# Expert rows scattered into a slot-sorted table, read back in column quarters and transposed on VectorE

## The reference

```python
def _moe_forward(hidden_states, Wg, W1, W2, W3, W1s, W2s, W3s):
    x = hidden_states.reshape(-1, D)
    shared = jax.nn.silu(x @ W1s.T) * (x @ W3s.T) @ W2s.T
    probs = jax.nn.softmax((x @ Wg.T).astype(jnp.float32), axis=-1)
    topk_w, sel = jax.lax.top_k(probs, TOP_K)                      # 4 of 16
    combine = jnp.zeros((T, E), x.dtype).at[jnp.arange(T)[:, None], sel].add(topk_w)
    h = jax.nn.silu(jnp.einsum('td,efd->etf', x, W1)) * jnp.einsum('td,efd->etf', x, W3)
    routed = jnp.einsum('etf,edf->td', h * combine.T[:, :, None], W2)
    return (shared + routed).reshape(B, S, D)

x = x + tanh(g_xattn) * attention(layernorm(x), ctx, wq, wk, wv, wo)
x = x + tanh(g_ffn) * moe(layernorm(x), ...)
```

## Time and profile before

| | us |
|---|---|
| median of 3 runs | 1171.72 (1171.42 to 1180.43) |
| the profiled execution's own time | 1170.14 |
| its span, first to last instruction | 1168.5 |
| attention, up to about | 436 |
| routing, about | 436 to 552 |
| experts, about | 552 to 1051 |
| combining, from about | 1051 |

### The profile page before, as it was taken

How to read it: one execution, slowest core, us unless ns; L and a number is a source line. 1 busy time by engine, 2 the same in 40 slices (tenths; PEclk the granted TensorE clock), 3 DMA queues, 4 the chain that set the end, 5 groups by cost and what they waited for, 6 DMA issues and landing times. The chain is left out here.

```text
span 1168.5 us, 18611 instructions
## 1 busy us (share of the span) xinstructions
PE 1106.2 (95%) x5666; PEld 940.0 (80%) x5667; DVE 490.0 (42%) x994; ACT 279.6 (24%) x575; POOL 477.5 (41%) x521
## 2 busy tenths in 40 slices
PE   3999999999999959998989999999999999988997
PEld 3888878878878827686879999999999999977775
DVE  2243463445336255996222222222222222225847
ACT  1231131122113002111223333333333333321210
POOL 4720201201100235101665565556656665617763
PEclk9999999999999968899999999999999999998999
DMA  9411320312220528133864666666666666627785
GB/s 348 193 73 73 122 94 1 141 74 72 108 72 0 225 85 297 36 111 96 325 226 162 216 229 229 238 220 222 236 220 229 229 220 229 215 69 237 226 278 162
DMA packets 54209, 199.70 MB, mean 171 GB/s; under 512 B 7009, under 2 KB 7009, under 8 KB 45985
## 3 DMA queue, kind: packets, MB, share of 16 engines
q0 software_dynamic: 21184, 122.44, 30.1%
q1 hardware_dynamic: 22624, 57.98, 13.9%
q10 hardware_dynamic: 10368, 18.88, 4.3%
HBM read 161.51 MB, written 37.75 MB: 171 GB/s over the span
## 5 line engine op out<-in xcount | busy, mean ns | idle before, releaser
L86 PE MATMUL c_ps_u<-expert_hi,xT_hi 128*128 x576 | 192.7, 335 | 2.0 <-DVE xT_lo L1445 1.9
L86 PE MATMUL c_ps_u<-expert_hi,xT_lo 128*128 x576 | 186.0, 323 | 0.0
L86 PE MATMUL c_ps_u<-expert_lo,xT_hi 128*128 x576 | 185.6, 322 | 0.0
L986 POOL TENSOR_TENSOR expert_lo<-expert_raw,expert_hi (+3 forms) x39 | 158.2, 4079 | 19.9 <-issue 14.0
L73 POOL TENSOR_TENSOR idle<-idle 128x1 f32<-128x1 f32 x91 | 17.5, 192 | 232.0 <-PE c_ps_x L1471 141.3
L86 PEld LDWEIGHTS c_ps_u<-expert_hi,xT_hi 128*128 128x128 f32 x576 | 108.8, 189 | 2.9 <-issue 2.9
L86 PEld LDWEIGHTS c_ps_u<-expert_lo,xT_hi 128*128 128x128 f32 x576 | 109.3, 190 | 0.0
L1459 DVE TENSOR_TENSOR hf<-c_ps_u,gate 128x352 f32<-128x352 f32 x72 | 37.8, 525 | 170.3 <-ACT gate L1434 170.3
L86 PEld LDWEIGHTS c_ps_u<-expert_hi,xT_lo 128*128 128x128 f32 x576 | 108.7, 189 | 0.0
L1449 DVE TENSOR_TENSOR hT_lo<-c_ps_h,hT_hi 128x256 fp32r<-128x256 f32 x72 | 30.6, 425 | 181.4 <-ACT hT_hi L1424 181.4
L86 PE MATMUL c_ps_y<-expert_hi,hT_hi 128*128 (+1 forms) x216 | 91.7, 425 | 2.6 <-DVE hT_lo L1450 2.3
(11 more groups left out here) (268 smaller groups left out, 2454.5 us busy)
## 6 DMA issues: line engine op xcount, KB each, us to landing
expert_hi<-we POOLq DMA_DIRECT2D x16, 1920.0 KB, 7.9
expert_raw<-we POOLq DMA_DIRECT2D x14, 1920.0 KB, 13.0
y_dram<-y ACTq DMA_DIRECT2D x72, 256.0 KB, 2.1
ctxT_hi<-ctxT POOLq DMA_DIRECT2D x4, 1024.0 KB, 7.4
ctxT_raw<-ctxT SPq DMA_DIRECT2D x4, 1024.0 KB, 5.6
ctx_raw<-ctx SPq DMA_DIRECT2D x4, 1024.0 KB, 4.8
r_t<-x SPq DMA_DIRECT2D x4, 1024.0 KB, 5.3
ctx_hi<-ctx POOLq DMA_DIRECT2D x4, 1024.0 KB, 6.9
```

What stands on the lines that cost most here:

```text
L86: last = pe.matmul(out, a[i], b[j], start=(n == 0), stop=(n == 3 * len(pairs) - 1))
L986: last = eng.tensor_tensor(lo, raw, hi, ALU.subtract)
```

## The change

- **A sorted table.** The DRAM tensor `sorted` has a row for every slot. In the attention phase SP fills it with copies of `x` from DRAM to DRAM (24 DMAs of 448 rows, 6 per batch), so that unused slots hold numbers. In the routing phase SP loads the 12 row tiles that are not on the chip yet, and POOL scatters all 2048 rows to their 4 slots each: 64 indirect DMAs. The one-hot matrices, the 64 matmuls and `index` are gone; `counts` and the choice of slots move up in `work`.
- **Loads.** SP, not POOL, brings the tile: 4 DMAs of 32 partitions x 4 x 128 columns, one for each quarter of the columns, after a wait for the whole scatter. The first four tiles are loaded at the end of the routing block, later ones in the expert block behind the zeros. W1 and W3 are laid out to match (`sides`).
- **Transposes.** VectorE transposes 32x32 blocks of `xg` into the new SBUF tile `xt`. ScalarE and VectorE split from `xt` instead of PSUM, one tile ahead (`high(t + 1)`, `low(t + 1)`). PE's `turn` is gone.
- **POOL in the loop** has only the weights' work. Its subtraction is as before one of 3840 columns and one of 512; a wait for `held` comes before it.

```diff
@@ attention_phase, SP
+            def fill(k):
+                for n in range(FILLS):
+                    sp.dma_start(sorted_d[k, n], io["x"][0:SORTED // (B * FILLS)]).then_inc(keep["filled"], 16)
...
                 stores(b - 1)
+                fill(b - 1)
...
+            fill(B - 1)
             sp.wait_ge(m_ready, 22 * B - 10)
@@ routing_phase, SP
             for i in range(IT):
                 sh.load(sp, 1, i)
+            for tile, at in rows.items():
+                if tile // IT != 1:
+                    sp.dma_start(at[:], xn2_d[tile]).then_inc(rows_in, 16)
...
-            sp.wait_ge(keep["gathered"][0], 16)
+            sp.wait_ge(moved, NT * TOPK * 16)
+            sp.wait_ge(sh.u_ready, 2 * SC)
+            for t in range(QUAD):
+                load_tile(sp, mem, later, t, t, keep["loaded"][t])
             load_expert(sp, later.w_raw, WE, io, 1, keep["second_raw_in"])
@@ routing_phase, POOL
+            def move(tile):
+
+                for q in range(TOPK):
+                    pool.indirect_dma_start(mem["sorted"], bass.IndirectOffsetOnAxis(
+                        ap=keep["slots"][:, tile, q:q + 1], axis=0), rows[tile][:], None).then_inc(moved, 16)
+
+            pool.wait_ge(slots_ready, 1)
+            pool.wait_ge(keep["filled"], B * FILLS * 16)
+            for i in range(IT):
+                pool.wait_ge(sh.xs_in[1][i], 16)
+                move(IT + i)
+            pool.wait_ge(rows_in, (NT - IT) * 16)
+            for tile in range(NT):
+                if tile // IT != 1:
+                    move(tile)
+            pool.wait_ge(scheduled, 1)
             pool.wait_ge(sh.t_free, 2 * IT)
-            pool.wait_ge(hot_ready, 1)
+            pool.wait_ge(moved, NT * TOPK * 16)
             load_expert(pool, later.w_hi, WE, io, 1, keep["w_in"])
...
@@ routing_phase, VectorE
-            work = {0: lambda: (rank(), choices()), 1: rest_of_down, 3: counts,
...
+            work = {0: lambda: (rank(), choices()), 1: rest_of_down, 2: counts, 3: slots, 5: weights, 7: schedule,
+                    8: lambda: places(range(BUFFERS)), 9: lambda: (turns(), done())}
@@ load_tile, new
+def load_tile(sp, mem, later, t, v, sem):
+
+    side = P // SIDE
+    tile = mem["sorted"].rearrange("(t g i) (a c) -> t a i g c", g=side, i=SIDE, a=side)[t]
+    for a in range(side):
+        sp.dma_start(later.xg[v][a * SIDE:(a + 1) * SIDE, :, :], tile[a]).then_inc(sem, 16)
@@ expert_phase, SP, behind the zeros
+            with sp.Fori(1, last + 1) as i:
+                for v in range(QUAD):
+                    sp.wait_ge(x_turned, i * QUAD + v - (QUAD - 1))
+                    load_tile(sp, mem, later, i * QUAD + v, v, loaded[v])
@@ expert_phase, POOL, step
-                pool.wait_ge(x_turned, t + 1)
-                pool.wait_ge(column_ready, t + 1)
-                hold(nc, nc.gpsimd, keep)
-                gather(v, column[v][:])
...
                     pool.wait_ge(w_in, e * 64 + 32)
+                    if later_than(t, 0):
+                        pool.wait_ge(held, e)
                     split_expert(pool, later, base, w_ready)
@@ expert_phase, ScalarE, step
-                turn(t, u)
                 if later_than(t, 1):
                     take(t - 2, (v - 2) % QUAD)
                 if later_than(t, 0):
                     turn_h(t - 1, 1 - u)
+                high(t + 1, 1 - u)
                 act.wait_ge(u_ready, t + 1)
@@ expert_phase, VectorE
+            def turn(t, v):
+                dve.wait_ge(loaded[v], (t + (QUAD - v)) * 16)
+                wait(dve, x_split, t)
+                dve.transpose(xt[:].rearrange("p k (g i) -> p g k i", i=SIDE),
+                              xg[v][:].rearrange("p g (k j) -> p g k j", j=SIDE)).then_inc(x_turned, 1)
+
+            def low(t, u):
                 dve.wait_ge(x_hi, t + 1)
-                dve.tensor_tensor(x[u][1][:], ps_x[:], x[u][0][:], ALU.subtract).then_inc(x_split, 1)
+                dve.tensor_tensor(x[u][1][:], xt[:], x[u][0][:], ALU.subtract).then_inc(x_split, 1)
...
-                turn(t, u)
+                turn(t + 1, (v + 1) % QUAD)
                 if later_than(t, 0):
                     turn_h(t - 1, 1 - u)
+                low(t + 1, 1 - u)
                 dve.wait_ge(gate_ready, t + 1)
@@ expert_phase, TensorE, step
-                turn(t, v)
                 if later_than(t, 1):
                     down(t - 2, u, bases[v - 2] if v >= 2 else place(t - 2))
```

More of the change, by code:

```diff
@@ L1398, in step, with high @@
                     pass
[L1400 to L1401 removed]
             pool.wait_ge(keep["second_raw_in"], 32)
[L1403 to L1405 removed]
+            tiles(pool, step)
         @block.scalar
         def _(act):
[L1409 removed]
+            def high(t, u):
                 act.wait_ge(x_turned, t + 1)
[L1411 removed]
+                act.activation(x[u][0][:], xt[:], ACT.Copy).then_inc(x_hi, 1)
             def take(t, v):
@@ L1465, in _ @@
         def _(pe):
-            def turn(t, v):
-                pe.wait_ge(gathered[v], (t + (QUAD - v)) * 4)
-                wait(pe, x_split, t)
-                for k in range(DC):
-                    last = pe.transpose(ps_x[:, k, :], xg[v][:, k * P:(k + 1) * P], keep["ident"][:])
-                last.then_inc(x_turned, 1)
             def weights(base, start, n, rows=P):
```

145 lines of the change are left out of this document (56 added, 89 removed).

## The result

The changed kernel takes 1259.67 us (median of 4 runs, 1242.02 to 1270.26), the kernel before 1173.01 us beside it: a ratio of 1.063, 95% interval 1.051 to 1.075. The forecast was 1207.0 us within 1170 to 1238: the direction holds, the size does not, and the time lies above the range. Both ratios compare fast runs alone, which leaves out two of the first four (1265.07 and 1270.26, over 1.5% above the fastest); the two medians stand at 1.074.

What follows compares the result with a forecast made beforehand. PE was taken to bound the expert block (busy 487.20 of 498.60 us); 1170.1 - 31.5 + 44 + 6 - 3 + 18 + 3 = 1206.6, some 1207 beside a median, range 1170 to 1238.

Steps and rivals of the forecast that it cites:

- Bound and transposes: Expert block: PE is the bound; removing its transposes saves 0.44 a tile over 72 tiles, -31.5 us, step 6.26.
- early loop: Start of the expert loop: a 6.0 us wait and slow stretch goes, but tiles may be late by 3: -3 us.
- Low part against the split: Expert loop: VectorE's two-SBUF-operand subtraction waits for POOL's 3840-column instruction, 15 stalls of mean 2.92: +44 us, bounds 0 to 91.
- the clock: Expert loop: stalls over 4 us drop PE's granted clock to 0.50, four at 1.45: +6 us, range 0 to 15.
- the two readings of the earlier trace: Expert loop: VectorE waits for one POOL piece and then runs (first), or until POOL's whole row of pieces is through.
- third rival: Expert loop: VectorE gets in only after both POOL pieces, stalls 63 and clock +10: 1229.6 us; 17 in 100.
- the second: Rival, expert loop: no exclusive wait between VectorE and POOL, so no stalls: 1156.6 us, faster; 8 in 100.
- The blocks' change: Routing to experts: 64 scatters then tile loads put the first product at about 573 instead of 555.04: +18 us.
- a sign of being wrong: Routing to experts: a first product before 565 or after 590 would show the forecast wrong.
- Attention +3: Attention: the table's fill delays a load by up to 8 us, twice: +3 us, range 0 to 16.

Runs made afterwards that it cites:

- e1: Changed kernel with POOL's split of an expert in the loop in 512-column pieces instead of one of 3840 and one of 512: 1163.23 us beside 1176.05 before.
- first profile: Profiled execution of the changed kernel in its first set of runs, the shortest of the four: 1242.02 us.
- e7: Changed kernel again, unedited, on a second chip: 1253.73 us, ratio 1.069 to the kernel before.
- e2: Changed kernel with 16 scatters in place of 64, only each token's first choice filled (outputs not the reference's): 1192.8 us.
- e3: Changed kernel with a wait after every four scatters until they have landed: 1243.32 us.
- e5: Changed kernel with seven more GpSimd instructions, waits met at once, behind each split in the loop, split left whole: 1270.16 us.
- e16: Kernel before, with the low part of the tile's rows in the loop subtracting two SBUF operands instead of reading PSUM: 1228.17 us beside 1173.85.
- groups 2, 3 and 5: Three of the five groups of follow-up runs, each on a different chip; the 512-column-pieces kernel took 1201.40, 1201.53 and 1217.14 us there.
- groups 1 and 4: The other two groups of follow-up runs, each on a different chip; the 512-column-pieces kernel took 1163.23 and 1162.50 us there.
- e17: Kernel of e1 (512-column pieces), unedited, as control in group 4: 1162.50 us.
- e19: Kernel of e1 (512-column pieces), unedited, as control in group 5: 1217.14 us.
- e9: Kernel of e1 (512-column pieces), unedited, as control in group 3: 1201.53 us.

## Why the prediction was right in direction and wrong in size

- **Bound and transposes: right.** In e1 two successive transposes of the hidden rows start 6.25 us apart (702.83, 709.08), forecast 6.26 against 6.70 in the earlier trace rows. With the early loop the block lost 36.8 us, forecast 31.5 + 3 = 34.5. VectorE's transpose, taken as 0.7 within 0.52 to 2.8, took 0.70 and cost nothing.
- **Low part against the split: right in mechanism, and in the sum; the sum partly by luck.** Forecast 44 + 6 for the clock. Against the 457.4 us without stalls the block of the whole split was longer by 35.2 (first profile), 51.1 (e7), 53.2 (e2), 50.7 (e3) and 66.5 (e5): a mean of 51.3, all within the forecast's bounds. But the waits for `hf` were 25.9, 36.2, 37.7, 36.6 and 45.0 us, a mean of 36.3 where 44 was forecast, and the lower clock took the rest: in these blocks it stood at 0.50 for 21.8 to 56.2 us against 7.2 in e1. Half of the difference, 7.3 to 24.5 us, is lost, a mean of 14.6 where 6 was forecast. The two errors offset each other. Between the two readings of the earlier trace rows the first was right: at 753.74 the low part got in between the 3840-column piece and the small one. The third rival falls, and with e16 so does the second. That is the rule of the Trainium skill (SBUF — State Buffer, section Who interferes with whom) as the forecast gave it, and VectorE's transpose, with one operand in SBUF, was indeed never held (0.71 us at most).
- **The blocks' change: here the prediction failed.** The step was "The blocks' change: +18", with "+10 to +34" as its bounds. It was made from POOL's and SyncE's terms alone. It asked when the scatter ends, and not what 64 scatters in a row do to the engines beside it; PE's own work up to 549 us was taken as untouched, and so was the work of ScalarE and VectorE that PE needs. PE was through at 612.54. Measured +72 (70.5 by the start of the first product, 555.04 to 625.50), which the forecast had itself named as a sign of being wrong (a first product after 590). Of the 49.5 us that are over the forecast 576 (573 and attention's 3), 42.6 are the slow stretch: the same kernel with pieces has its first product at 582.9 and 582.0 without it, at 619.1, 620.5 and 627.3 with it. (The two compared profiles are from different groups.) Without it the first profile would have been at about 1199 us (1242.0 - 42.6, an estimate), near the forecast; the whole split with all 64 unpaced scatters was never run on a chip without the stretch. The gathers of the earlier trace rows, from which the 1.26 was taken, did not show it.
- The other 7 us of that step: the slots came at 481.4 instead of 478, the last scatter landed at 566.2, and in e1 from SyncE's last load (576.3) to the next block's first instruction (580.6) there are 4.3 us, forecast 0.5. Timeline of SyncE and POOL in e1:

```profile
566.93 8.34 SPq L1297 DMA_DIRECT2D xg<-sorted_dram  x16
575.85 0.44 SPq L983 DMA_DIRECT2D expert_raw<-we_rest  x1
580.57 0.52 POOL L1371 MEMSET zeros<- 128x512 f32 x1 [11.88 <-POOLq L1014]
```

- What was missed besides: SyncE's tile loads stand behind its last store of the routing block. With PE late, its lateness is therefore followed by another 13 us (612.54 to 625.50) instead of running beside the loads.
- **Attention +3: wrong by its sign, and small.** Routing began 1.9 us earlier, at 434.07; in all other runs of the changed kernel at 431 to 436. The fill is hidden.
- The sum, from the profiled execution's 1242.0: the forecast 1206.6, + 49.5 (change of blocks), - 17.0 (loop: -1.5 and not +15.5), + 3.0 (the end, of which no experiment was made) = 1242.1. The median of 1259.7 lies higher as the loop's stalls vary from build to build and run to run.

## What stays open

Why a long unbroken stream of GpSimd's indirect DMAs holds back TensorE, ScalarE and VectorE on some chips (that of the first result, and those of groups 2, 3 and 5) and not on others (groups 1 and 4). No two groups were made on the same chip, so chip and session are not told apart, nor was the length of the pause varied. All these are executions with a recorded trace; whether the stretch is there without recording, no run says. That it is the fetching of instructions is argued, not shown: PE was slowed in the middle of a run of equal matmuls, with no semaphore in sight, 21 to 28 us after the stream began: in the eight profiles with a stretch the first gap opens at 502 to 509 us, and the stream began at 477.6 to 482.7. The Trainium skill (Runtime: NRT & Kernel Launch, section Instruction fetch mechanics) says that an engine fetches its next block of instructions by a DMA queue of its own while it works on the present one; that would fit a point in the code at which it runs dry. The traces agree that there is such a queue: their packets of the kind "instruction" on q8 are of 16 KB, one to about 120 of PE's matmuls. In time such packets are indeed late: from 505 to 563 us e17, without the stretch, has two of them, and e19, with it, none.

```profile
q8 instruction: 2, 0.03, 0.3%
```

But they can be late because PE is, and the first gap doesn't come at one point of PE's code: it opens 170 to 203 matmuls ahead of the routing block's last. And in e9 the packet came at 513.24, in the midst of the stretch, and PE's pace did not come back: 22 matmuls in the 47.5 us behind it.

```profile
515.50:563.00 47.50, 11.38 (x22) 6.20 (x22) 0.69 (x1) 0.60 (x1) 36.21 (x38) 0.53 0.54 209
```

So one late packet on PE's queue isn't the whole cause, and what holds ScalarE is open as well: in seven of the eight profiles it first takes up a product 4 to 10 us behind the last indirect DMA, in e9 9 us before it and the second 9 us behind it.

## What to carry to other kernels

Price a new stream of DMAs not only by its own end, but ask which engines must keep going beside it; a long unbroken run of indirect DMAs from GpSimd can hold the others for as long as it lasts, on some chips. A pause of 3 us after every four cured that, but the longer stream ate the gain: the better use of the finding is to issue fewer such DMAs in a row, or to put them where nothing waits (not tried here). When an operand moves from PSUM to SBUF on VectorE, look at GpSimd: a subtraction of two SBUF operands waits for the end of a whole GpSimd instruction, so cut those short (nine pieces of 1.3 us cost nothing here, one of 8.5 us cost 35 to 67 us over 15 uses). Compare variants only in runs on the same chip: the same kernel took 1162.5 and 1217.1 us.

## What the runs showed of the hardware that was not expected

- In an unbroken stream of GpSimd's indirect DMAs, 1.28 us apart, TensorE's matmuls of 512 columns came up to 2.8 us apart instead of 0.23, at a granted clock of 0.50 (520 to 540 us), ScalarE left finished products lying for over 60 us (492.01 to 571.49 without an instruction), and VectorE stood for 16 us. Scatters did it on three of the five chips of the groups, gathers on the one of these on which they were tried. Stores outstanding at a DMA share of 0.89, with GpSimd idle, did not.
- A break filled by 2.95 us of small fills, or a waited landing, after every four takes it away (one run each, beside a control with it).
- Stalls cost more than their own length: in e16 39.0 us of waits made the block 60.2 us longer, in e7 36.2 us made it 51.1 longer. Most of the rest is the clock, which stood at 0.50 for 62.5 us of the block in e16 and for 34.2 in e7, against 6.5 and 7.2 in the blocks that they are compared with: half of the difference is 28 and 13.5 us.
